# Attention steps of a transformer layer on one core: projections placed earlier, one sum of four key tiles in place of two sums of pairs, the shift behind a pair block

## The chip, the core and the metric

One core of a Trainium2 chip runs the kernel as one program. The metric is the device time in microseconds. TensorE (PE) multiplies matrices, VectorE (DVE), ScalarE (ACT) and GpSimd (POOL) do elementwise work, SyncE (SP) issues most transfers. Each engine has a queue of its own and works it off in order; they wait for each other by semaphores.

## The reference

```python
# x: 2 x 1024 x 512; 16 heads of 32; FF = 2048
qkv = einsum('bsd,ed->bse', x, w_qkv) + b_qkv
scores = einsum('bhqd,bhkd->bhqk', q, k) / sqrt(32) + causal
out = einsum('bhqk,bhkd->bhqd', softmax(scores), v) @ w_out.T + b_out
x = layernorm(x + out)
hidden = relu((x @ sign(up_w).T) * up_scale)
x = layernorm(x + (hidden @ sign(down_w).T) * down_scale * output_scale)
```

## The kernel before

The attention goes in 8 steps (`STEPS`): a step is one group of four heads of one batch, so that step s is batch s % 2, group s // 2. In a step there are 48 score tiles (`PIECES`): for each half f of the queries (512), each key tile j of 128, each of the four heads h. Piece n = 4g + h belongs to key-tile group g; groups 0 to 3 are the first half, 4 to 11 the second. Groups 4 to 7 are full tiles of 512 columns; those of 0 to 3 and 8 to 11 touch the diagonal, narrow from 512 to 128 columns and are masked.

For every piece PE writes scores into PSUM (L983), ACT takes the exponential into a ring of 14 tiles, `probs` (L681), GpSimd masks diagonal tiles (L594). Per group, PE multiplies the four tiles with V (`pv`, L1013) and with ones for the row sums (`sum`, L1007); these use 32 columns of the array each, four heads side by side, and a pair of groups makes a "pair block". For groups 4 to 7 GpSimd first adds tiles in pairs (`add`, L601: groups 4+5 into `pairs`, then 6+7) and PE sums the pairs (`sum_added`, L991): two blocks of four heads per step. VectorE then divides (`norm`, L805 a reciprocal, L807 a product), and the second half's first `pv` (group 4) waits for the first half's division.

Softmax needs a maximum per row beforehand. For step s+1, 48 unit scores (`max`, L946) are computed during step s, into three banks `ps_unit`, and reduced by VectorE: units 16 to 31 by L783 (512 columns each), the others by L779 with the causal mask. Unit n waits until unit n-3 is reduced. The maxima are turned by PE (`shift`, L957), ACT and VectorE split them into a high and low part (L666, L793), SyncE lays them as two rows beside K for the scores of step s+1.

Q and K of a coming step come from 4 projections of 12 matmuls (`proj`, L906), in fp32r with values split into a high and a low part: `PARTS` lists weight and input part of the three passes. In steps from 2 on every projection goes into one bank, `ps_proj`. ACT copies it out twice (`full` L654, `high` L660), GpSimd forms the low part (L588), SyncE stores and reloads. The first matmul of a projection waits until `high` of the one before is done. In even steps VectorE and GpSimd also prepare the weights of the next group (L767, L567).

What sets the order on all engines is one list written out by hand, `plan()`. Every job has a slot; 48 slots make a step, and slot t+n is score n. All engines walk the same sorted list, each taking its own kinds of jobs. `PAIRED` and `ALONE` (last two steps) place the groups, `MAXIMA` the unit scores, `BLOCK` and `LAST_BLOCK` the projections: (steps ahead, projection, first slot, slots between matmuls, slots of evict, keep and fill). The score of piece n waits until the exponential of piece n-2 is done, since there are two score banks.

In the last step PE also begins the output projection (`attn`, L1029); the feed-forward part (L1056, L1073) begins behind the last scores.

The waits of the parts that the prediction walks through:

```python
# PE, proj
if m == 0:
    wait(pe, s_qk, NB * s + k - (s == 0 or s == 1 and k == 1))
# PE, max
wait(pe, s_max, NU * s + n - 2)
# ACT, shift
act.wait_ge(s_mt, 2 * s + n + 1)
# ACT, high
nc.scalar.activation(parts[:, k % 2, 0, :], proj_bank(s, n)[:, :], ...).then_inc(s_qk, 1)
# PE, pv
if what == "pv" and j == 0:
    wait(pe, s_norm, QT * s + 4 * f)
```

## Time and profile before

| | |
|---|---|
| three runs | 795.46, 795.60, 797.47 us, median 795.6 |
| profiled execution, its own time | 801.23 us |
| its span, first to last instruction | 799.5 us |
| mean granted clock of TensorE | 0.974 |
| PE, DVE, ACT, POOL busy | 746.0, 456.0, 323.2, 345.9 us |
| shares of the chain that ended last | PE 75%, DVE 15%, issue 4% |

In a timeline row the first number is the start from the beginning of the span, the second how long the merged instructions lasted, then engine, line, operation, what is written and read, the shape and the count; in brackets the idle time of the engine just before and who ended it. Ends of matmuls are modelled, so starts are what to go by.

### The profile page before, as it was taken

To read this page: it belongs to the slowest core of one execution; us is meant where nothing else is said; L and a number is where in the kernel's file an instruction comes from. 1 tells how busy PE (TensorE), PEld (TensorE's weight loads), DVE (VectorE), ACT (ScalarE), POOL (GpSimd) and SP (SyncE) were. 2 spreads that over 40 slices of the span, in tenths; PEclk is the share of its full clock that TensorE was granted. 3 is DMA by queue.
4 is the path that set the end of the run, shared out by engine and by line. 5 is a ranking of instruction groups with operands and counts; after the bars stand their busy time and mean duration, and the time that the engine had idled before them with its cause. 6 is when DMAs were issued, how large, how long until landed. Compare 5 with 4: busy or idle time off the path is not lost.

```text
span 799.5 us, 11694 instructions
## 1 busy us (share of the span) xinstructions
PE 746.0 (93%) x4048; PEld 509.6 (64%) x4048; DVE 456.0 (57%) x1086; ACT 323.2 (40%) x631; POOL 345.9 (43%) x479
## 2 busy tenths in 40 slices
PE   6899899999999999999989897999999999999994
PEld 4687655655556455555554453588778877878882
DVE  3276386676766767758576662433277329433614
ACT  5111355555555655545555556532231223221220
POOL 4441456364553555544527534362244234323333
PEclk9999899999999999999997997999999999999998
DMA  6966263525545344344467440413002101000101
GB/s 233 311 166 184 68 178 114 146 81 144 156 112 157 95 134 145 92 145 124 130 188 219 145 162 5 155 43 119 14 14 105 27 14 39 14 1 2 52 1 52
DMA packets 44619, 85.71 MB, mean 107 GB/s; under 512 B 4880, under 2 KB 13584, under 8 KB 44432
## 3 DMA queue, kind: packets, MB, share of 16 engines
q1 hardware_dynamic: 35536, 79.72, 33.1%
q10 hardware_dynamic: 9024, 5.24, 2.3%
q8 instruction: 32, 0.52, 0.3%
q14 instruction: 27, 0.22, 0.1%
HBM read 55.33 MB, written 29.36 MB: 106 GB/s over the span
## 4 chain that ended last, share of the span: by engine, by line
PE 75%; DVE 15%; issue 4%; ACT 2%; DMA 2%; POOL 2%; ACTq 0%; SPq 0%; POOLq 0%; DVEq 0%
PE ps_heads L1013 9%; PE ps_unit L946 9%; PE ps_proj L906 8%; DVE heads_sb L805 7%; PE ps_proj L1056 7%; PE ps_score L983 6%; PE ps_score L1073 6%; PE ps_unit L1029 6%; PE ps_unit L1056 5%; PE ps_sum L1007 5%; PE ps_heads L1073 3%; PE ps_sum L1073 3%; DVE maxes L783 2%; PE ps_sum L991 2%; DVE heads_sb L807 2%
## 5 line engine op out<-in xcount | busy, mean ns | idle before, releaser
L681 ACT ACTIVATE probs<-ps_score 128x512 f32<-128x512 f32 (+3 forms) x360 | 170.8, 490 | 180.1 <-PE ps_score L983 171.3
L779 DVE CUSTOM_DVE_ANT_0 ps_unit<-ps_unit,causal 128x128 f32<-128x128 f32 (+3 forms) x256 | 121.9, 512 | 77.0 <-PE ps_unit L946 74.3
L625 POOL TENSOR_TENSOR hid_low<-hid_raw,hid_high 128x512 fp32r<-128x512 f32 x64 | 85.0, 1328 | 174.6 <-DVE hid_high L856 171.5
L946 PE MATMUL ps_unit<-stack 96*128 96x512 f32 (+3 forms) x384 | 134.4, 364 | 10.9 <-DVE maxes L783 4.3
L983 PE MATMUL ps_score<-stack 98*128 98x512 f32 (+2 forms) x360 | 134.9, 383 | 7.5 <-ACT probs L681 6.0
L594 POOL TENSOR_SCALAR_AFFINE_SELECT probs<-probs 128x128 f32<-128x128 f32 x256 | 73.9, 294 | 153.6 <-ACT probs L681 150.9
L946 PEld LDWEIGHTS ps_unit<-stack 96*128 96x128 f32 x384 | 72.6, 193 | 57.3 <-issue 17.4
L856 DVE CAST hid_high<-hid_raw 128x512 fp32r<-128x512 f32 x64 | 27.1, 424 | 131.1 <-ACT hid_raw L736 130.9
L783 DVE TENSOR_REDUCE maxes<-ps_unit 128x1 f32<-128x512 f32 x128 | 80.7, 684 | 26.0 <-PE ps_unit L946 25.6
L983 PEld LDWEIGHTS ps_score<-stack 98*128 98x128 f32 x360 | 69.3, 195 | 40.6 <-ACT probs L681 23.9
L1013 PE MATMUL ps_heads<-probs,v_rows 128*32 128x512 f32 (+3 forms) x768 | 84.5, 511 | 5.1 <-DVE heads_sb L807 3.3
L601 POOL TENSOR_TENSOR pairs<-probs 128x512 f32<-128x512 f32 x64 | 79.9, 1278 | 10.2 <-ACT probs L681 9.4
L805 DVE RECIPROCAL heads_sb<-ps_sum 128x128 f32<-128x128 f32 x64 | 60.8, 950 | 12.1 <-PE ps_sum L1007 12.1
L588 POOL TENSOR_TENSOR parts<-qk_full,parts 128x512 fp32r<-128x512 f32 x32 | 41.1, 1283 | 57.2 <-ACT parts L660 57.2
L736 ACT ACTIVATE hid_raw<-ps_proj,up_scale 128x512 f32<-128x512 f32 x32 | 22.0, 688 | 93.0 <-PE ps_proj L1056 93.0
L906 PE MATMUL ps_proj<-x_high,w_high 128*128 128x512 f32 x116 | 46.0, 425 | 6.5 <-ACT x_high L638 6.5
L1073 PE MATMUL ps_score<-down_sb,hid_high 128*128 128x512 f32 x124 | 50.1, 404 | 0.0
L1007 PE MATMUL ps_sum<-probs,ones 128*32 128x128 f32 (+3 forms) x512 | 49.4, 441 | 0.0
L1073 PE MATMUL ps_score<-down_sb,hid_low 128*128 128x512 f32 x124 | 48.9, 395 | 0.0
L906 PE MATMUL ps_proj<-x_low,w_high 128*128 128x512 f32 x116 | 45.3, 417 | 0.0
L1013 PEld LDWEIGHTS ps_heads<-probs,v_rows 128*32 128x32 f32 x768 | 19.6, 110 | 39.6 <-issue 24.8
L906 PE MATMUL ps_proj<-x_high,w_low 128*128 128x512 f32 x116 | 44.7, 416 | 0.0
(184 smaller groups left out, 1208.1 us busy)
## 6 DMA issues: line engine op xcount, KB each, us to landing
stack<-qk_parts SPq DMA_DIRECT2D x96, 256.0 KB, 4.7
qk_parts<-parts SPq DMA_DIRECT2D x32, 512.0 KB, 2.7
v_all<-h_even ACTq DMA_DIRECT2D x16, 256.0 KB, 3.4
v_rows<-v_all SPq DMA_DIRECT2D x8, 512.0 KB, 4.5
heads_t<-heads_sb SPq DMA_DIRECT2D x16, 256.0 KB, 2.6
raw<-up_w SPq DMA_DIRECT2D x8, 512.0 KB, 3.6
x_tile<-x_rows SPq DMA_DIRECT2D x16, 256.0 KB, 5.0
raw<-down_w SPq DMA_DIRECT2D x8, 512.0 KB, 3.8
```

What stands on the lines that cost most here:

```text
L625: nc.gpsimd.tensor_tensor(hid[1][:, (HM * s + n) % 3, :], hid_raw[:, n % 2, :], hid[0][:, (HM * s + n) % 3, :].bitcast(FP32), ALU.subtract ...
L681: nc.scalar.activation(probs[:, (NP * s + n) % RING, 0:width], score_bank(s, n)[:, off:off + width], ACT.Exp, scale=SCALE).then_inc(s_exp, 1)
L779: nc.vector.tensor_tensor_reduce(ps_unit[n % 3][:, 0:width], ps_unit[n % 3][:, 0:width], causal[:, HALF - width:], 1.0, NEG, ALU.add, ALU.max,
L783: nc.vector.tensor_reduce(maxes[:, 1, col:col + 1], ps_unit[n % 3][:, :], AXIS_X, ALU.max).then_inc(s_max, 1)
L805: nc.vector.reciprocal(heads_sb[:, cols], ps_sum[:, cols]).then_inc(s_rc, 1)
L906: mm = nc.tensor.matmul(proj_bank(s, k)[:, :], ws[wp][:, c, t, :], xs[xp][:, c, t0:t0 + HALF], start=(m == 0), stop=(m == 11))
L946: nc.tensor.matmul(ps_unit[n % 3][:, 0:width], stack[s % 2][0:96, 1, f, h, i % 4 * P:(i % 4 + 1) * P], stack[s % 2][0:96, 0, c, h, 0:width ...
L983: nc.tensor.matmul(score_bank(s, n)[:, 0:width + off], stack[s % 2][0:98, 0, j // 4, h, j % 4 * P:(j % 4 + 1) * P], stack[s % 2][0:98, 1, ...
L1007: nc.tensor.matmul(ps_sum[rows, at:at + width], ones[:, :], tile, **args).then_inc(s_pv, 1)
L1013: mm = nc.tensor.matmul(ps_heads[rows, at:at + width], v_rows[:, s % 2, j, rows], tile, **args)
L1056: mm = nc.tensor.matmul(ps_up[n % 2][:, :], up_sb[n // 8][:, n % 8, m % DC, :], turned[s % 2][m // DC][:, m % DC, :], start=(m == 0), stop ...
L1073: mm = nc.tensor.matmul(ps_down[i][:, :], hid[part][:, (HM * s + n) % 3, i * P:(i + 1) * P], down_sb[:, down_at(n), :], start=(n == 0 and ...
```

## The change

Projections (1, 2) and (2, 0) begin at slots 0.5 and 20.5 instead of 4.2 and 22, with more room between their matmuls. From step 1 on, the pass with the weights' low part is the last of three. The unit scores 16 to 18 start at slot 26.3 instead of 25.2, and those behind them are spread anew. The shift moves from 35.9 to 36.02, behind the pair block at 36, and stays ahead of `full` at 36.05. In steps 0 to 5 GpSimd adds groups 4 to 7 into one set of four tiles, `added`, in 12 instructions from slot 21.7 on, and PE sums them in one block at slot 43.9, which now starts the sum of the second half. Steps 6 and 7 have no adds: groups 4 to 7 are summed directly there, each beside its `pv`.

```diff
--- before.py
+++ after.py
@@ -39,17 +39,19 @@
 ALONE_NORM = [[18.4, 18.41, 18.42, 18.43, 50.4, 50.41, 50.42, 50.43],
               [17.6, 17.61, 17.62, 17.63, 48.7, 48.71, 48.72, 48.73]]
 
-MAXIMA = ([10.2 + 0.55 * u for u in range(5)] + [13.4 + 0.55 * u for u in range(11)]
-          + [25.2 + 0.6 * u for u in range(5)] + [28.4 + 0.7 * u for u in range(27)])
-BLOCK = [(1, 2, 4.2, 0.72, 13.05, 15.8, 18.5), (1, 3, 13.3, 0.5, 19.65, 22.4, 24.8),
-         (2, 0, 22, 1.1, 36.05, 38.8, 41.3), (2, 1, 36.3, 0.6, 44.05, 46.8, 49.2)]
-LAST_BLOCK = [(1, 2, 4.2, 0.48, 9.9, 12.5, 14.9), (1, 3, 11.9, 0.45, 17.1, 19.9, 22.2)]
+MAXIMA = ([10.4 + 0.5 * u for u in range(5)] + [13.4 + 0.55 * u for u in range(11)]
+          + [26.3 + 0.6 * u for u in range(3)] + [28.4 + 0.53 * u for u in range(14)] + [37.5 + 0.66 * u for u in range(15)])
+BLOCK = [(1, 2, 0.5, 0.98, 13.05, 15.8, 18.5), (1, 3, 13.3, 0.5, 19.65, 22.4, 24.8),
+         (2, 0, 20.5, 1.25, 36.05, 38.8, 41.3), (2, 1, 36.3, 0.6, 44.05, 46.8, 49.2)]
+LAST_BLOCK = [(1, 2, 0.5, 0.78, 9.9, 12.5, 14.9), (1, 3, 11.9, 0.45, 17.1, 19.9, 22.2)]
 
 
 FIRST_ADD, LAST_ADD = 4, 8
-NA = 2 * GH
+NA = 3 * GH
+ADDING = STEPS - 2
 
 
 UNITS = [(h, i, c) for f in range(2) for c in range(f + 1) for h in range(GH) for i in range(4 * f, 4 * f + 4)]
@@ -141,12 +143,12 @@
         paired = s < STEPS - 2
         for g, at in enumerate(PAIRED if paired else ALONE[s % 2]):
             put(t + at, "pv", s, g)
-            if g < FIRST_ADD or g >= LAST_ADD:
+            if g < FIRST_ADD or g >= LAST_ADD or s >= ADDING:
                 put(t + at, "sum", s, g)
-        for a in range(2):
-            for h in range(GH):
-                put(t + 25.6 + 8 * a + 0.01 * h, "add", s, GH * a + h)
-            put(t + (33, 41)[a], "sum_added", s, a)
+        if s < ADDING:
+            for a in range(NA):
+                put(t + 21.7 + 1.3 * a, "add", s, a)
+            put(t + 43.9, "sum_added", s)
         for q, at in enumerate(PAIRED_NORM if paired else ALONE_NORM[s % 2]):
             put(t + at, "norm", s, q)
             if q % 4 == 3:
@@ -154,7 +156,7 @@
         if s + 1 < STEPS:
             for u, at in enumerate(MAXIMA):
                 put(t + at, "max", s + 1, u)
-            put(t + 35.9, "shift", s + 1, 0)
+            put(t + 36.02, "shift", s + 1, 0)
             put(t + 47.2, "row_max", s + 1, 1)
             put(t + (51.9 if s + 2 < STEPS else 48.2), "shift", s + 1, 1)
             put(t + 17, "v_rows", s + 1)
@@ -274,8 +276,8 @@
         s_mask = sem("probs_masked")
         s_pv = sem("probs_used")
         s_rc = sem("row_sum_inverted")
-        s_add = sem("prob_pairs_added")
-        s_used = sem("prob_pairs_used")
+        s_add = sem("probs_added")
+        s_used = sem("added_probs_used")
         s_norm = sem("heads_normalized")
         s_st = [sem(f"heads_stored{f}") for f in range(2)]
         s_raw = [sem(f"raw_weights_loaded{i}") for i in range(2)]
@@ -337,7 +339,7 @@
         stack1 = sb(left, "stack1", [P, 2, 2, GH, HALF], FP32R)
         stack = [stack0, stack1]
         probs = sb(left, "probs", [P, RING, HALF], FP32)
-        pairs = sb(left, "pairs", [P, GH, HALF], FP32)
+        added = sb(left, "added", [P, GH, HALF], FP32)
         v_rows = sb(left, "v_rows", [P, 2, QT, P], FP32)
         heads_sb = sb(left, "heads_sb", [P, HALF], FP32)
         causal = sb(left, "causal", [P, HALF], BF16)
@@ -594,12 +596,17 @@
                     nc.gpsimd.affine_select(out=tile, in_=tile, compare_op=ALU.is_ge, fill=0.0, base=0,
                                             pattern=[[1, P]], channel_multiplier=-1).then_inc(s_mask, 1)
                 if what == "add":
-                    k = NP * s + GH * (FIRST_ADD + n // GH * 2) + n % GH
-                    pool.wait_ge(s_exp, k + GH + 1)
-                    wait(pool, s_used, NA * s + n - GH + 1)
-                    nc.gpsimd.tensor_tensor(pairs[:, n % GH, :], probs[:, k % RING, :], probs[:, (k + GH) % RING, :],
-                                            ALU.add).then_inc(s_add, 1)
+                    h = n % GH
+                    k = NP * s + GH * (FIRST_ADD + 1) + n
+                    pool.wait_ge(s_exp, k + 1)
+                    if n < GH:
+                        wait(pool, s_used, GH * s - GH + h + 1)
+                        other = probs[:, (k - GH) % RING, :]
+                    else:
+                        pool.wait_ge(s_add, NA * s + n - GH + 1)
+                        other = added[:, h, :]
+                    nc.gpsimd.tensor_tensor(added[:, h, :], other, probs[:, k % RING, :], ALU.add).then_inc(s_add, 1)
                 if what == "sign" and n < 2:
 
                     pool.wait_ge(s_sign, n + 1)
@@ -676,8 +683,8 @@
 
                     wait(act, s_pv, NP * s + n - RING + 1)
                     k = n - RING - GH * FIRST_ADD
-                    if 0 <= k < 2 * NA:
-                        act.wait_ge(s_add, NA * s + k // (2 * GH) * GH + k % GH + 1)
+                    if s < ADDING and 0 <= k < GH * (LAST_ADD - FIRST_ADD):
+                        act.wait_ge(s_add, NA * s + (k if k < GH else k - GH) + 1)
                     nc.scalar.activation(probs[:, (NP * s + n) % RING, 0:width], score_bank(s, n)[:, off:off + width],
                                          ACT.Exp, scale=SCALE).then_inc(s_exp, 1)
                 if what == "sign":
@@ -889,7 +896,7 @@
                 if what == "proj":
                     k, m = n // 12, n % 12
                     t, f = PROJ[k]
-                    (wp, xp), c = PARTS[m // DC], m % DC
+                    (wp, xp), c = PARTS[m // DC if m < DC or s == 0 else 3 - m // DC], m % DC
                     b, g = s % 2, s // 2
                     t0 = b * SEQ + f * HALF
                     if b == 0 and k == 0 and m == 0:
@@ -987,8 +994,8 @@
                 if what == "sum_added":
                     for h in range(GH):
                         rows = slice(h * HD, (h + 1) * HD)
-                        pe.wait_ge(s_add, NA * s + GH * n + h + 1)
-                        nc.tensor.matmul(ps_sum[rows, :], ones[:, :], pairs[:, h, :], start=(n == 0), stop=False,
+                        pe.wait_ge(s_add, NA * s + NA - GH + h + 1)
+                        nc.tensor.matmul(ps_sum[rows, :], ones[:, :], added[:, h, :], start=True, stop=False,
                                          tile_position=(0, h * HD)).then_inc(s_used, 1)
                 if what in ("pv", "sum"):
                     f, j, _ = PIECES[GH * n]
@@ -1011,7 +1018,7 @@
                         else:
                             pe.wait_ge(s_exp, NP * s + k + 1)
                         mm = nc.tensor.matmul(ps_heads[rows, at:at + width], v_rows[:, s % 2, j, rows], tile, **args)
-                        if FIRST_ADD <= n < LAST_ADD:
+                        if s < ADDING and FIRST_ADD <= n < LAST_ADD:
                             mm.then_inc(s_pv, 1)
                 if what == "attn":
                     i, m = n // 12, n % 12
```

## Rows read from the trace of the kernel before

**Rows 1.** The page, busy time of each engine (share of span, instructions).

```profile
PE 746.0 (93%) x4048; PEld 509.6 (64%) x4048; DVE 456.0 (57%) x1086; ACT 323.2 (40%) x631; POOL 345.9 (43%) x479
```

**Rows 2.** Windows: us, then busy of each engine, clock, DMA share, GB/s.

```profile
98.00:149.10 51.10, 48.39 (x326) 28.66 (x322) 36.28 (x101) 27.72 (x59) 26.93 (x48) 1.00 0.47 135
404.70:455.00 50.30, 43.81 (x250) 22.91 (x247) 34.26 (x91) 26.46 (x52) 25.14 (x36) 0.88 0.64 205
455.00:505.00 50.00, 43.88 (x262) 22.35 (x261) 20.38 (x37) 28.71 (x54) 19.72 (x36) 0.88 0.23 76
416.00:419.50 3.50, 2.14 (x5) 0.74 (x4) 3.40 (x7) 3.29 (x7) 0.49 (x1) 1.00 0.72 291
419.50:429.80 10.30, 9.62 (x29) 4.68 (x30) 5.20 (x11) 4.14 (x8) 7.66 (x5) 0.50 0.71 204
498.00:501.40 3.40, 3.37 (x12) 1.08 (x12) 0.00 (x0) 0.00 (x0) 0.95 (x4) 0.50 0.00 0
```

**Rows 3.** Timeline of TensorE, step 3 and start of step 4: start us, us, line.

```profile
261.50 0.73 PE L983 MATMUL ps_score<-stack 98*128 98x512 f32 x2
...
267.22 0.50 PE L946 MATMUL ps_unit<-stack 96*128 96x512 f32 x1 [0.71 <-DVE maxes L783]
...
268.48 1.92 PE L1013 MATMUL ps_heads<-probs,v_rows 128*32 128x512 f32 x16
...
274.32 1.07 PE L991 MATMUL ps_sum<-pairs,ones 128*32 128x512 f32 x8
...
278.03 0.28 PE L957 MATMUL ps_unit<-ident,maxes 128*16 128x128 f32 x1 [0.56 <-DVE maxes L783]
...
278.42 1.92 PE L1013 MATMUL ps_heads<-probs,v_rows 128*32 128x512 f32 x16
...
280.43 0.45 PE L906 MATMUL ps_proj<-x_high,w_high 128*128 128x512 f32 x1
...
287.51 1.07 PE L1013 MATMUL ps_heads<-probs,v_rows 128*32 128x512 f32 x8
...
293.17 0.99 PE L983 MATMUL ps_score<-stack 98*128 98x512 f32 x2 [0.26 <-ACT probs L681]
...
295.64 0.44 PE L983 MATMUL ps_score<-stack 98*128 98x384 f32 x1
...
301.03 0.50 PE L946 MATMUL ps_unit<-stack 96*128 96x512 f32 x1 [0.30 <-DVE maxes L779]
```

**Rows 4.** Timeline of ScalarE, the same stretch.

```profile
262.03 3.46 ACT L681 ACTIVATE probs<-ps_score 128x512 f32<-128x512 f32 x6
...
278.40 0.27 ACT L666 ACTIVATE shift_h<-ps_unit 16x128 fp32r<-16x128 f32 x1 [0.54 <-PE ps_unit L957]
...
279.52 0.66 ACT L660 ACTIVATE parts<-ps_proj,bias_sb 128x512 fp32r<-128x512 f32 x1
```

**Rows 5.** Timeline of VectorE, the same stretch.

```profile
266.48 3.07 DVE L783 TENSOR_REDUCE maxes<-ps_unit 128x1 f32<-128x512 f32 x5
270.87 4.42 DVE L783 TENSOR_REDUCE maxes<-ps_unit 128x1 f32<-128x512 f32 x7 [1.32 <-PE ps_unit L946]
...
293.00 0.17 DVE L789 TENSOR_TENSOR row_max<-maxes 128x16 f32<-128x16 f32 x1
...
300.63 0.29 DVE L779 CUSTOM_DVE_ANT_0 ps_unit<-ps_unit,causal 128x128 f32<-128x128 f32 x1
```

**Rows 6.** Timeline of GpSimd in step 7.

```profile
492.75 4.99 POOL L601 TENSOR_TENSOR pairs<-probs 128x512 f32<-128x512 f32 x4
```

**Rows 7.** Timeline of TensorE in step 6.

```profile
420.18 1.94 PE L1013 MATMUL ps_heads<-probs,v_rows 128*32 128x512 f32 x8 [1.62 <-DVE heads_sb L807]
```

**Rows 8.** Timeline of TensorE in step 7.

```profile
498.03 1.30 PE L1013 MATMUL ps_heads<-probs,v_rows 128*32 128x512 f32 x2 [1.74 <-POOL probs L594]
```

**Rows 9.** Timeline of all engines, end of step 6.

```profile
450.80 1.26 POOL L619 TENSOR_TENSOR x_tile<-x_tile,b_out_sb 128x512 f32<-128x512 f32 x1
450.87 1.23 DVE L789 TENSOR_TENSOR row_max<-maxes 128x16 f32<-128x16 f32 x1
```

## The prediction

> **What bounds it now.** I read the page first: TensorE is busy 93% of the span [rows 1]. So a change pays only where it shortens TensorE's queue, or a wait in front of it. By stretches, the eight attention steps fall in two kinds [rows 2]: steps 0 to 5 take 51.1 us each, PE busy 48.4 of it at full clock; step 6 (404.7 to 455) and step 7 (455 to 505) have PE busy 44 of 50 at a mean clock of 0.88. The feed-forward half behind 507 us isn't touched. Everything below is therefore one period of step 3, walked along TensorE's timeline, times the number of steps, and then steps 6 and 7 by themselves. Slots are those of plan(); slot 20 of step 3 is at 261.50, slot 28's pair block at 268.48, slot 36's at 278.42, slot 44's at 287.51, slot 52's ends at 295.64 [rows 3].
>
> What the reader is to see in that walk is who ends each wait. From 261.50 to 268.48 (6.98 us) scores go at ScalarE's pace, six exponentials in 3.46 us [rows 4], and then a maximum waits 0.71 for VectorE, which has only just finished the division (its first reduce starts at 266.48) [rows 3, 5]. At 278.03 the shift waits 0.56 for VectorE. Between 287.51 and 302 it is ScalarE at 293.17 and VectorE at 301.03 [rows 3].
>
> **The change, part by part, one period.**
>
> Sums. A block of column sums of the added tiles takes 1.07 us at 274.32 [rows 3]; with a slower matmul on both sides I take 1.2 for it (bounds 1.0 and 1.3). Two blocks become one in steps 0 to 5: 1.2 less. GpSimd gets twelve adds for eight; four take 4.99 us [rows 6], so 15.0 us, begun at slot 21.7 and over by slot 36 to 38. The block at slot 43.9 (some 286 us) and the exponentials 30 to 45, which reuse the tiles, come later, so this costs nothing; if GpSimd were late, each add behind its need would cost 1.25. The projection parts behind them on its queue and on SyncE's go out at about the time they do now.
>
> Slots 20 to 28. Two maxima leave this stretch and the first comes 1.1 slots later, so the 0.71 is gone. ScalarE's chain stays: seven exponentials at 0.577 from 262.03 end at 266.1. The first projection now sits behind score 20 and must wait for the bank until ScalarE's copy, just ahead of 262.03, is done, which holds score 21 back 0.3 or so. The pair block then starts at about 267.0 instead of 268.48: 1.5 less (bounds 1.0 and 2.0). In even steps the weight copy and the low weights come ahead of this as before; passing them last only makes them due later, and I cost it at nothing; without that cover it would be one short wait per group.
>
> Slots 28 to 36. TensorE comes to the maxima with only three done. Thirteen reduces of 0.63 (seven take 4.42, [rows 5]) are left, 8.2 us, against about 6.7 us of matmuls. VectorE has an idle stretch under the pair block, its next reduce starts near 269.7, and the last but one of the maxima is let in at about 276.1. Slot 36's block starts near 277.05, so this stretch is 10.0 us against 9.94: the sum block's 1.2 and the 0.56 are eaten by waits for VectorE.
>
> Slots 36 to 44. Here lies what decides. The shift now comes behind the pair block (1.85 us), at about 278.9. ScalarE has one queue in the same order: shift_h, then the copy of the finished projection (36.05), then its high part (36.1). Now these run under the pair block: 278.40, and the high part from 279.52 for 0.66, and the next projection's first matmul is at 280.43, just after [rows 3, 4]. After the change that first matmul stands right behind the shift, and waits for the same bank. From shift to the end of the high part is 0.37+0.18+0.57+0.7, so 1.9 us with the signal, of which 0.2 is the shift's own: 1.7 us of TensorE doing nothing (bounds: nothing, if something else had held it anyway, and 2.0). Behind it are scores 37 on, all in order. The rest, 7.08 from 280.43 to 287.51, loses one maximum (0.23). So 1.85+1.9+6.95 against 9.09: 1.6 more.
>
> Slots 44 to 61. One maximum of 512 columns has moved in here (0.23), and the third after it waits for its reduce of 0.63, about 0.3 more. Four projections fill the gaps between scores 0 to 3; those are latency gaps of about 0.9 in all, so they cost some 0.3: 0.8 more up to slot 52. From the end of slot 52's block the division and the next unit on VectorE set the time: the fourth maximum comes 5.39 after it (295.64 to 301.03, VectorE's unit from 300.63) [rows 3, 5] however little stands in between. Taking four projections out of that stretch only makes a larger hole; one fewer behind it gives 0.24. Net 0.55 more (bounds −0.5 and 1.2).
>
> Sum: −1.5+0.1+1.6 = +0.2 for slots 20 to 44, six times, +1.2; +0.55 five times, +2.8. At the start of step 0 there is no division, so there the fill is a true gain of about 0.9.
>
> Step 6. Its entry has five projections ahead of the slot-52 block, +1.1 by the same walk. It regains direct sums, four blocks; the first two fall where the clock is at 1.2 GHz (one block of eight took 1.94 there, [rows 7]) and cost 1.9 each, the others half of that, 0.9, less 2.4 for the two added sums: +3.2 if TensorE has no room, 0 if all of it goes into waits for VectorE. I take 1.8. Step 7: the first direct sum lies in a wait, the other three cost 3.6 (1.9, 0.9 and 0.9, rounded down); 2.4 goes; and the masks no longer stand behind four adds [rows 6]: the 1.74 at 498.03 goes [rows 8], and with it, if the clock stays up, half of the 3.4 us at clock 0.50 behind it [rows 2], 1.7. With 0.2 of smaller slack that is −2.4 (3.6−2.4−1.7−1.7−0.2; bounds 0 and −5).
>
> All: +1.2+2.8−0.9+2.9−2.4 = **+3.6 us**. The profiled execution took 801.2 (span 799.5); that is 5.6 above the median of the runs, 795.6. I carry the difference over: 799.2.
>
> **Rivals.** (a) *The bank wait doesn't show.* If the first matmul behind the shift isn't held, six times 1.7 = 10.2 goes, and 789.0 is left: faster. For it: the other terms of the period, a block and two VectorE waits, are visible gains. Against: ScalarE's order and the bank are the plan's own. It decides at the gap between shift and next projection; below 1.1 us the whole is faster than before. (b) *The clock falls.* It fell behind 416 to 419.5, where PE had little to do, and stood at 0.50 for 10.3 us [rows 2]. The holes ahead of the fourth maximum and behind the shift are each 1.5 to 1.7 long; now no steady step loses its clock. The shortest stretch at 0.50, 498.0 to 501.4, costs half its length, 1.7; one such in each of six steps gives 809. It decides if PE's work around a hole gets as thin as there. (c) *Gains and losses cancel*: the small terms (0.3s and 0.2s) come out 0.6 less per step, and the time is 795.6. (d) *VectorE blocked by the adds.* A row_max took 1.23 us beside a GpSimd add, and 0.17 alone [rows 5, 9]; were it caught in each of six steps, 1.06 each, 805.6. Against: the adds end ten slots before it, and reduces took 0.61 to 0.63 beside adds and without.
>
> The Trainium skill, "SBUF — State Buffer", section "Who interferes with whom", has a rule that speaks against more GpSimd adds: a VectorE instruction with two SBUF inputs and a GpSimd instruction that reads SBUF shut each other out for the whole instruction, while a tensor_reduce never does. By that rule the sum stays as it is unless row_max drifts into the adds, and then it is (d)'s; the trace agrees, both in the long row_max and in the even reduces.
>
> **Numbers.** Forecast as summed: 0.43, its own range 795 to 803, a fifth of it within 0.3% of before. (a) 0.30; (b) 0.14; (c) 0.11; (d) 0.02. A change under 0.3% (2.4 us) can't be told from none. Faster 0.30; within 0.3%: 0.20; slower 0.50. The range, from (a) with some more of step 7 to (b): 786 to 809.
>
> **What would show it.** Right: after slot 36's block a shift, then an idle time of TensorE of 1.5 to 1.9 us ended by ScalarE's high part; one L991 block a step; no wait at slot 26; waits for L783 spread over slots 29 to 35; a hole before the fourth maximum of over 1 us; a period of 51.7 to 52.1 us; step 7 without the mask wait. Wrong: a period at or below 50.5, or the projection starting within 0.5 us of the shift; also clock falls before 400 us.

## The result and the profile after

The changed kernel takes **803.3 us** (median of 4 runs, 802.42 to 803.91), the kernel before 795.77 in the same comparison (795.46 to 797.47): ratio 1.0089, 95% interval [1.0067, 1.0112]. It is 0.9% slower. The forecast was 799.2 in a range of 786 to 809, slower with 0.50: right in its sign and inside its range, 4.1 us too low.

The profiled executions stand closer together: 803.83 (span 802.1) against 801.23 (span 799.5). The page after, busy time of each engine:

```profile
PE 744.5 (93%) x4032; PEld 503.6 (63%) x4032; DVE 451.1 (56%) x1086; ACT 322.9 (40%) x631; POOL 356.5 (44%) x487
```

PE is *less* busy than in [rows 1], by 1.5 us and 16 instructions, and the kernel is slower: the loss is waiting. Windows after (us, busy of each engine, clock, DMA share, GB/s), of step 0, step 3, steps 6 and 7, then of the three low stretches in them:

```profile
86.70:136.20 49.50, 46.78 (x282) 27.38 (x283) 29.91 (x89) 27.44 (x57) 33.53 (x52) 1.00 0.42 124
239.90:291.70 51.80, 48.45 (x316) 28.22 (x315) 35.21 (x100) 27.77 (x58) 29.22 (x48) 1.00 0.42 123
395.40:457.50 62.10, 54.18 (x332) 26.33 (x331) 38.43 (x105) 31.82 (x64) 18.35 (x37) 0.90 0.59 184
457.50:509.60 52.10, 46.78 (x306) 25.07 (x304) 21.60 (x41) 31.81 (x62) 12.35 (x33) 0.92 0.25 82
404.40:407.90 3.50, 3.26 (x16) 0.60 (x16) 0.83 (x5) 0.12 (x1) 1.41 (x3) 0.52 0.58 221
421.50:428.30 6.80, 5.25 (x20) 1.69 (x21) 2.54 (x6) 2.14 (x4) 2.35 (x1) 0.51 0.79 211
455.60:465.90 10.30, 9.03 (x47) 5.44 (x40) 3.15 (x9) 3.74 (x7) 5.09 (x8) 0.51 0.06 14
```

The same windows of before for steps 0, 6 and 7:

```profile
87.00:138.60 51.60, 48.93 (x290) 30.01 (x290) 30.65 (x88) 27.51 (x57) 28.23 (x48) 0.93 0.39 115
394.20:450.00 55.80, 51.27 (x316) 27.12 (x315) 38.76 (x105) 32.12 (x64) 27.75 (x46) 0.91 0.67 208
450.00:507.20 57.20, 48.46 (x290) 25.00 (x288) 22.64 (x41) 31.98 (x62) 22.59 (x43) 0.88 0.22 74
```

Cut at the first score of each step (read off TensorE's timeline; step 7 ends at its last score), the difference of the two profiled executions is:

| | step 0 | steps 1 to 5, all | step 6 | step 7 |
|---|---|---|---|---|
| before | 51.68 | 255.57 | 55.79 | 57.21 |
| after | 49.46 | 259.22 | 62.12 | 52.09 |
| difference | −2.2 | +3.65 | +6.3 | −5.1 |
| forecast | −0.7 | +3.75 | +2.9 | −2.4 |

(Steps 1 to 5 of the forecast are +0.75 each, 0.2+0.55; step 0 is 0.2−0.9; step 6 is 1.1+1.8.) The steady steps came out as forecast, the three odd ones with the right sign and at half the size or less. What the forecast's walk through step 3 named stands in TensorE's timeline after:

```profile
275.68 0.39 PE L990 MATMUL ps_score<-stack 98*128 98x384 f32 x1
276.00 1.92 PE L1020 MATMUL ps_heads<-probs,v_rows 128*32 128x512 f32 x16
277.86 0.28 PE L964 MATMUL ps_unit<-ident,maxes 128*16 128x128 f32 x1
279.69 0.73 PE L913 MATMUL ps_proj<-x_high,w_high 128*128 128x512 f32 x2 [1.56 <-ACT parts L667]
...
285.30 1.06 PE L998 MATMUL ps_sum<-added,ones 128*32 128x512 f32 x8
```

Against [rows 3]: the shift (now L964) stands behind the pair block, and behind it TensorE does nothing for 1.56 us until ScalarE has made the high part. There is one block of added sums (L998) for two. ScalarE's timeline shows the queue that does it:

```profile
278.23 0.27 ACT L673 ACTIVATE shift_h<-ps_unit 16x128 fp32r<-16x128 f32 x1 [1.62 <-PE ps_unit L964]
278.41 0.66 ACT L661 ACTIVATE qk_full<-ps_proj,bias_sb 128x512 f32<-128x512 f32 x1
278.98 0.66 ACT L667 ACTIVATE parts<-ps_proj,bias_sb 128x512 fp32r<-128x512 f32 x1
```

ScalarE itself waits 1.62 for the shift's transpose, with two finished projection tiles to copy queued behind. VectorE's timeline of the same stretch:

```profile
265.67 1.88 DVE L790 TENSOR_REDUCE maxes<-ps_unit 128x1 f32<-128x512 f32 x3
268.73 7.87 DVE L790 TENSOR_REDUCE maxes<-ps_unit 128x1 f32<-128x512 f32 x13 [1.19 <-PE ps_unit L953]
```

Three reduces before the pair block, thirteen behind it, as the walk had it ([rows 5]: five and seven). And in the page's list of costliest groups the wait is one row:

```profile
L913 PE MATMUL ps_proj<-x_high,w_high 128*128 128x512 f32 x116 | 46.2, 424 | 16.2 <-ACT parts L667 9.3
```

9.3 us of it ended by L667, six times 1.55.

### The profile page after: what moved, and what is told of

Same layout as the page of the kernel before. It is cut to its first block, busy times and chain, and to the rows that moved or that the text cites. A ratio compares the mean times of both kernels' runs of the same rounds, so it can differ in the third digit from the quotient of the medians.

```text
span 802.1 us, 11678 instructions
## 1 busy us (share of the span) xinstructions
PE 744.5 (93%) x4032; PEld 503.6 (63%) x4032; DVE 451.1 (56%) x1086; ACT 322.9 (40%) x631; POOL 356.5 (44%) x487
## 4 chain that ended last, share of the span: by engine, by line
PE 76%; DVE 12%; issue 4%; ACT 3%; DMA 2%; POOL 1%; SPq 0%; ACTq 0%; DVEq 0%; POOLq 0%
PE ps_heads L1020 9%; PE ps_unit L953 9%; PE ps_proj L913 8%; PE ps_score L990 7%; PE ps_proj L1063 7%; PE ps_score L1080 6%; PE ps_unit L1036 6%; PE ps_sum L1014 5%; PE ps_unit L1063 5%; DVE heads_sb L812 4%; PE ps_heads L1080 3%; PE ps_sum L1080 3%; DVE maxes L790 2%; PE ps_sum L933 1%; PE ps_score L933 1%
## 5 line engine op out<-in xcount | busy, mean ns | idle before, releaser
L688 ACT ACTIVATE probs<-ps_score 128x512 f32<-128x512 f32 (+3 forms) x360 | 170.3, 491 | 183.1 <-PE ps_score L990 176.3
L953 PE MATMUL ps_unit<-stack 96*128 96x512 f32 (+3 forms) x384 | 133.7, 366 | 14.5 <-DVE maxes L786 10.2
L1020 PE MATMUL ps_heads<-probs,v_rows 128*32 128x512 f32 (+3 forms) x768 | 82.0, 505 | 4.3 <-DVE heads_sb L814 4.3
L609 POOL TENSOR_TENSOR added<-added,probs 128x512 f32<-128x512 f32 x48 | 60.5, 1274 | 0.0
L1014 PE MATMUL ps_sum<-probs,ones 128*32 128x512 f32 (+3 forms) x576 | 58.0, 468 | 0.0
L743 ACT ACTIVATE hid_raw<-ps_unit,up_scale 128x512 f32<-128x512 f32 x32 | 21.9, 685 | 52.8 <-PE ps_unit L1063 52.8
```

What stands on the lines that cost most here:

```text
L688: nc.scalar.activation(probs[:, (NP * s + n) % RING, 0:width], score_bank(s, n)[:, off:off + width], ACT.Exp, scale=SCALE).then_inc(s_exp, 1)
L953: nc.tensor.matmul(ps_unit[n % 3][:, 0:width], stack[s % 2][0:96, 1, f, h, i % 4 * P:(i % 4 + 1) * P], stack[s % 2][0:96, 0, c, h, 0:width ...
L1014: nc.tensor.matmul(ps_sum[rows, at:at + width], ones[:, :], tile, **args).then_inc(s_pv, 1)
L1020: mm = nc.tensor.matmul(ps_heads[rows, at:at + width], v_rows[:, s % 2, j, rows], tile, **args)
```

## The experiments

Each was timed beside the kernel before (medians 795.3 to 796.0 over 16 to 29 runs). Step lengths are those of its profiled execution. Rows of different comparisons are best set against each other by their ratios.

| kernel | us | ratio to before | step 0 | steps 1 to 5, mean | step 6 | step 7 |
|---|---|---|---|---|---|---|
| before | 795.77 | 1 | 51.68 | 51.11 | 55.79 | 57.21 |
| after | 803.3 | 1.0089 [1.0067, 1.0112] | 49.46 | 51.84 | 62.12 | 52.09 |
| e1_shift_late | 793.49 | 0.9953 [0.9926, 0.9980] | 48.04 | 50.42 | 59.63 | 53.46 |
| e2_proj_back | 805.77 | 1.0103 [1.0066, 1.0139] | 52.09 | 52.07 | 62.00 | 52.22 |
| e3_only_shift | 802.35 | 1.0076 [1.0049, 1.0104] | 52.31 | 51.99 | 54.41 | 57.00 |
| e4_only_sums | 790.3 | 0.9918 [0.9883, 0.9954] | 49.61 | 50.31 | 56.29 | 53.47 |
| e5_sums_maxima | 799.04 | 1.0030 [1.0001, 1.0060] | 50.90 | 51.23 | 61.06 | 52.38 |
| e6_sums_fill | 791.54 | 0.9931 [0.9904, 0.9959] | 47.78 | 50.28 | 56.39 | 53.46 |
| e7_parts_back | 803.15 | 1.0098 [1.0070, 1.0126] | 49.48 | 51.84 | 61.58 | 52.64 |
| e9_maxima_back_6 | 791.82 | 0.9937 [0.9911, 0.9963] | 48.03 | 50.42 | 57.80 | 51.83 |
| e11_shift_back | 792.61 | 0.9955 [0.9932, 0.9979] | 49.04 | 50.41 | 61.95 | 51.78 |
| e10_even_maxima | 797.13 | 1.0000 [0.9973, 1.0026] | 50.24 | 51.08 | 59.57 | 52.93 |
| e12_fill_wait | 794.16 | 0.9968 [0.9944, 0.9992] | 47.78 | 50.25 | 59.56 | 53.47 |

### The shift: the wait behind it

The changed kernel, with the shift a few places later, behind the copies' slots 36.05 and 36.1:

```diff
-            put(t + 36.02, "shift", s + 1, 0)
+            put(t + 36.2, "shift", s + 1, 0)
```

> The changed kernel with one slot altered: the shift at 36.2, behind ScalarE's two copies of the projection (36.05 and 36.1) and still ahead of the next projection (36.3). Theory (bank wait): TensorE's wait of 1.56 us for ScalarE's high part goes in each of steps 0 to 5, the period falls from 51.8 to about 50.3 us, and the time from 803.3 to 794 (792 to 796), at or below the kernel before. Rival (the wait is only passed on, to the shift's own chain or to VectorE, which stands at the maxima anyway): under 3 us are won, time above 800, and a new wait of over 1 us stands behind the pair block or ahead of score 48.

793.49 us. ScalarE now copies while the pair block runs, and in TensorE's timeline the projection follows the shift at once; all that is left is 0.15 for VectorE:

```profile
273.85 1.92 PE L1020 MATMUL ps_heads<-probs,v_rows 128*32 128x512 f32 x16
275.71 0.28 PE L964 MATMUL ps_unit<-ident,maxes 128*16 128x128 f32 x1
275.74 0.71 PE L913 MATMUL ps_proj<-x_high,w_high 128*128 128x512 f32 x2
...
276.78 0.39 PE L953 MATMUL ps_unit<-stack 96*128 96x256 f32 x1 [0.15 <-DVE shift_l L800]
```

A position in a list, 0.18 of a slot, is worth 9.8 us by the medians (1.4% by the two ratios, whose intervals lie far apart), and more than the whole loss; in the profiled executions 8.5 us of it lie in steps 0 to 5, 1.42 in each. The same slot put alone into the kernel before:

```diff
-            put(t + 35.9, "shift", s + 1, 0)
+            put(t + 36.02, "shift", s + 1, 0)
```

> The kernel before with the shift at 36.02 in place of 35.9 and nothing else. Theory (bank wait): the wait of 0.56 for VectorE ahead of the shift goes, and a wait of 1.5 to 1.7 for ScalarE's high part comes behind it: 0.9 to 1.1 more in each of steps 0 to 5, period 52.1, time 795.8 + 6 = 802 (800 to 803). Rival (the pair block hides the shift and nothing waits): 0.5 less per step, 792 to 793.

802.35 us, in the middle of what was expected, 6.3 more than the kernel before beside it; and the wait stands in its timeline too:

```profile
277.48 1.92 PE L1013 MATMUL ps_heads<-probs,v_rows 128*32 128x512 f32 x16
279.33 0.28 PE L957 MATMUL ps_unit<-ident,maxes 128*16 128x128 f32 x1
281.17 0.50 PE L906 MATMUL ps_proj<-x_high,w_high 128*128 128x512 f32 x1 [1.50 <-ACT parts L660]
```

Here the period grows by 0.88 only, since the wait for VectorE ahead of the shift (0.56 in [rows 3]) goes in return. In the changed kernel there is hardly such a wait to win (with the shift ahead of the block, below, it sums to 1.3 us over six steps), and so taking the bank wait out gives 1.42 a step.

### The sums alone

The changed kernel with MAXIMA, BLOCK, LAST_BLOCK, the order of the passes and the shift as before: only the twelve adds, the one block at slot 43.9 and the direct sums in steps 6 and 7 are new.

```diff
-            put(t + 36.02, "shift", s + 1, 0)
+            put(t + 35.9, "shift", s + 1, 0)
...
-                    (wp, xp), c = PARTS[m // DC if m < DC or s == 0 else 3 - m // DC], m % DC
+                    (wp, xp), c = PARTS[m // DC], m % DC
```

(and the three lists of slots back to those of before.)

> The kernel before with the sums alone changed: twelve adds and one block per step in steps 0 to 5, direct sums in steps 6 and 7; projections, maxima and shift stand as before. Theory (VectorE's reduces take a part of the saved block back): of the 1.2 us of a block 0.7 to 0.9 is won per step, period 50.3, step 6 some 2 longer, step 7 some 2 to 4 shorter, time 790 (788 to 793). Rival 1 (GpSimd's twelve adds are late, and score exponentials or the block at slot 43.9 wait for them): 796 or more, with waits for L609. Rival 2 (TensorE alone counts): 1.2 per step, 787 or less.

790.3 us, as expected: **the sums alone make the kernel 0.8% faster than before.** The period falls by 0.9 in steps 2 to 5 (50.2 for 51.1), by 0.5 in step 1. All of it lies between slots 28 and 36, 9.03 us for 9.93: the block that goes (1.07 in [rows 3]), less 0.14 that the wait for VectorE ahead of the shift grows (0.7 for 0.56). Its windows of steps 3, 6 and 7:

```profile
235.00:285.20 50.20, 47.38 (x315) 28.43 (x316) 35.67 (x100) 27.73 (x58) 29.19 (x49) 1.00 0.44 127
385.70:442.00 56.30, 50.48 (x331) 25.68 (x331) 38.42 (x106) 32.01 (x65) 17.99 (x39) 0.97 0.65 209
442.00:495.40 53.40, 46.73 (x309) 24.74 (x306) 22.81 (x43) 31.39 (x60) 13.31 (x34) 0.94 0.23 78
```

Step 6 is only 0.5 longer than before, but at a clock of 0.97 for 0.91. At 1.2 GHz it spent 3.4 us here and 10.2 before; half of the 6.8 less is 3.4, so at the same clock the direct sums cost step 6 up to 3.9 us. Step 7 is 3.7 shorter, 3.4 of which such a count gives to the clock too (6.8 us low for 13.6).

### The projection at the start of a step

```diff
-BLOCK = [(1, 2, 0.5, 0.98, 13.05, 15.8, 18.5), (1, 3, 13.3, 0.5, 19.65, 22.4, 24.8),
+BLOCK = [(1, 2, 4.2, 0.72, 13.05, 15.8, 18.5), (1, 3, 13.3, 0.5, 19.65, 22.4, 24.8),
...
-LAST_BLOCK = [(1, 2, 0.5, 0.78, 9.9, 12.5, 14.9), (1, 3, 11.9, 0.45, 17.1, 19.9, 22.2)]
+LAST_BLOCK = [(1, 2, 4.2, 0.48, 9.9, 12.5, 14.9), (1, 3, 11.9, 0.45, 17.1, 19.9, 22.2)]
```

> The changed kernel with projection (1, 2) begun at slot 4.2 again, in all steps. Theory (the division on VectorE sets slots 52 to 61): the hole of 1.26 us ahead of the fourth maximum shrinks to 0.3, the stretch from slot 44 to 61 loses 0.5 in steps 1 to 5 and 1.1 at step 6's entry, step 0 loses its gain of 0.9: 803.3 less 3, so 800 (798 to 802). Rival (the fill is a true gain, since it uses time in which scores wait for exponentials): the time rises by 3 to 6, to 806 to 809.

805.77 us: neither as expected; it lies nearer the rival's 806, but the two ratios overlap (1.0103 and 1.0089), and the rival's reason would show in every step. The projections' new place does not cost the steady steps (51.76 to 51.86 in four of the five, as after), so my theory of 0.5 a step falls. Step 0 loses what the fill gave it (52.09 for 49.46), and step 3 took 53.07 by a fall of the clock at its start. The window:

```profile
244.90:248.30 3.40, 3.40 (x35) 1.75 (x35) 0.42 (x2) 1.04 (x3) 0.69 (x3) 0.55 0.82 219
```

The next two kernels are the one with the sums, each with one more edit. With the fill (slot 4.2 to 0.5, both lists):

> The kernel with the new sums alone (790.3 us), with the projection of slot 4.2 begun at slot 0.5 in every step and the maxima, the other blocks and the shift as before. Theory (the fill pays only where nothing else ends the wait, in step 0): step 0 goes from 49.6 to about 48.0 us and loses its stretch of low clock, steps 1 to 5 stay at 50.25, steps 6 and 7 stay at 109.8: 788.7 (787.5 to 790). Rival (the fill is what costs in steps 6 and 7): these take 3 us more, 792 (791 to 793.5).

Steps as the theory had them (step 0 at 47.78, no low stretch in it; steps 1 to 7 unchanged), but the median, 791.54, lies above the expected 787.5 to 790 and can't be told from that of the sums alone: the intervals overlap almost wholly. The profiled execution, 788.08, was the best of its ten. With the maxima's new slots instead:

> The kernel with the new sums alone (790.3 us), with the maxima's new slots added to it and nothing else. Theory (the maxima's new slots are what costs steps 6 and 7): the steady period goes from 50.25 to about 50.5 us, five times 0.25 is 1.2, and steps 6 and 7 together go from 109.8 to about 113, so 790.3 + 1.2 + 3.2 = 794.7 (793 to 797). Rival (steps 6 and 7 lose by the projections filled in between the first scores, or by a clock fall that has nothing to do with the maxima): steps 6 and 7 stay within 1 us of 109.8, and the time is 790 to 792.

799.04 us, more than either expected. Steps 6 and 7 together rose to 113.4, as the theory said. But steps 1, 2 and 4 took 51.8 to 51.9, and steps 3 and 5 took 50.3: three of five began with a fall of the clock. The window of the first, then the 3.4 us ahead of it, and the same stretch of step 3, where no fall followed:

```profile
137.40:140.80 3.40, 3.26 (x35) 1.60 (x34) 0.28 (x1) 1.45 (x4) 0.88 (x3) 0.57 0.58 144
134.40:137.80 3.40, 2.70 (x10) 1.43 (x10) 2.71 (x11) 2.19 (x6) 1.33 (x5) 1.00 0.52 175
238.00:241.40 3.40, 2.70 (x10) 1.43 (x10) 2.69 (x11) 2.21 (x6) 1.35 (x5) 1.00 0.70 208
```

What TensorE did ahead of the first, in its timeline:

```profile
135.18 0.75 PE L952 MATMUL ps_unit<-stack 96*128 96x384 f32 x2 [0.38 <-DVE maxes L785]
135.77 2.43 PE L989 MATMUL ps_score<-stack 98*128 98x256 f32 x5
138.00 0.41 PE L963 MATMUL ps_unit<-ident,row_max 128*16 128x128 f32 x1
```

The merged row carries the shape of its first score alone: it is the last score of step 0 (256 columns) and the first four of step 1 (512 each). From the second on they start 0.53 to 0.64 us apart, while a matmul of 512 columns right behind another of 512 starts 0.24 behind it (281.60 and 281.84 in the changed kernel), so TensorE in part waits in them, though the row counts as busy. Then the full set of parts, with the shift alone where it was:

```diff
-            put(t + 36.02, "shift", s + 1, 0)
+            put(t + 35.9, "shift", s + 1, 0)
```

> The changed kernel with the shift alone back at slot 35.9, ahead of the pair block. Against the kernel with the new sums and the new maxima (799.0 us) it differs by the projections filled in at slot 0.5, by the first projection at slot 20.5 and by the order of the passes. Theory (the fill keeps PE fed at the start of a step, and so the clock up): no stretch of low clock at 136, 188 or 291 us, all of steps 1 to 5 at 50.4, step 0 at 48: 799.0 less 1.5 for each of four falls and less 1.3 of step 0 is 792 (790 to 794). Rival (the falls come with the maxima's new slots whatever stands at slot 0.5): periods of 51.8 in some of steps 1 to 5 again, and 796 to 800.

792.61 us, and steps 1 to 5 all at 50.35 to 50.48, with no low stretch in any. Step 0 did have one, 3.4 us at 87.9, and took 49.04 for the 48 expected: in step 0 the fill doesn't rule a fall out. The same place in its timeline has the projections between the scores:

```profile
134.72 0.52 PE L990 MATMUL ps_score<-stack 98*128 98x256 f32 x2
135.07 0.40 PE L913 MATMUL ps_proj<-x_high,w_high 128*128 128x512 f32 x1
135.36 0.50 PE L990 MATMUL ps_score<-stack 98*128 98x512 f32 x1
135.70 0.39 PE L913 MATMUL ps_proj<-x_high,w_high 128*128 128x512 f32 x1
```

So the fill is worth nothing in time where the clock holds, and 1.5 us a step where it would fall. The two kernels differ also in the first projection at 20.5 and the order of the passes; the run that differs from the changed kernel by the fill alone (e2_proj_back) had one fall in its five steady steps. Counted over all profiled executions: with the maxima's new slots and no fill, four of ten steady steps began with a fall; with these slots and the fill, none of 25; with the old slots and no fill, none of 20. In these executions a fall took both, the new slots and the missing fill; what in the slots brings it isn't shown.

### The maxima in step 6

```diff
-            for u, at in enumerate(MAXIMA):
+            for u, at in enumerate(MAXIMA if s + 2 < STEPS else LAST_MAXIMA):
```

with the shift at 36.2 and LAST_MAXIMA the list of before.

> The changed kernel with the shift at slot 36.2 (793.5 us), and in step 6 alone the maxima at their old slots. Theory (the maxima's new slots cost step 6 some 3.1 us between its slots 32 and 48, where VectorE also splits the attention's output in parts, and nothing in steps 1 to 5): step 6 takes 56.5 instead of 59.6, steps 1 to 5 stay at 50.4, step 7 at 53.5: 790.3 (789 to 792). Rival (step 6 is longer by its projections, or by where its clock falls): step 6 stays over 58.5 and the time at 792 to 795.

791.82 us, inside the expected range; step 6 takes 57.80 for 59.63. Both kernels have a low stretch of 6.8 us in that step, so this 1.8 is not the clock: from slot 28 to the end it is 24.9 us for 26.8. The size is 1.8 and not the 3.1 I had expected, and the medians' 1.7 lies within the noise of both intervals; the direction is the theory's. TensorE's waits from slot 28 of step 6 on, with the new slots (shift at 36.2):

```profile
PE ps_unit L953 <- DVE maxes L786: 2.5, 3, 1.2
PE ps_unit L953 <- DVE shift_l L800: 0.6, 1, 0.6
```

and with the old ones in that step:

```profile
PE ps_unit L955 <- DVE maxes L788: 1.5, 2, 1.3
PE ps_unit L955 <- DVE shift_l L802: 0.8, 1, 0.8
```

One wait of 1.0 for VectorE is visible; the rest of the 1.8 is not in the named waits.

### The order of the passes

```diff
-                    (wp, xp), c = PARTS[m // DC if m < DC or s == 0 else 3 - m // DC], m % DC
+                    (wp, xp), c = PARTS[m // DC], m % DC
```

> The changed kernel with the low weights' pass back in its old place, in the middle, in every step. Theory (the order of the three passes is worth nothing, since the low weights are ready long before either order needs them): the time of the changed kernel, 803.3 (801.5 to 805), and the same step lengths. Rival (the low weights came late in the old order): a wait of TensorE for GpSimd or VectorE ahead of the second pass in even steps, 0.5 us or more each, 805 to 808.

803.15 us, the changed kernel's time, with the same steady steps: the order is worth nothing, as costed.

### The kernel before once more

> The kernel before, unchanged, for a second profile of it. Theory (the first profiled execution, 801.2 us, was an unlucky one by its clock: stretches at half clock at 88, 420, 454, 481 and 498 us): this execution lies at 795 to 797, with less time at half clock in steps 0, 6 and 7, and steps 1 to 5 at 51.1 as before. Rival (profiling itself costs this kernel some 5 us): 801 again, with the same stretches.

803.36 us at a clock of 0.972. My theory fell: this execution has the same low stretches from step 0 to step 7 as the first, to their lengths (among them 6.8 us at 90, 10.2 at 421, 6.8 at 483), and the same step lengths to 0.04. How common that is, another comparison shows: of its 29 runs of before the median is 795.38 at a clock of 0.981, and seven lie between 800.39 and 802.32 at 0.974 to 0.976; over the four comparisons of the experiments 11 of 88 lie above 800. Two such in two may be chance or may be the profile; that is open. For other kernels the profiled execution lies on either side of their median (796.22 for 793.49, 788.08 for 791.54). What counts is the consequence, below.

### Two versions that were to beat both kernels

The sums with the fill, and in steps 0 to 5 an even pitch for the maxima, none ahead of slot 26.3:

```diff
-          + [25.2 + 0.6 * u for u in range(5)] + [28.4 + 0.7 * u for u in range(27)])
+          + [26.3 + 0.6 * u for u in range(3)] + [28.4 + 0.65 * u for u in range(29)])
```

> A version that might beat both kernels: the new sums, the projection begun at slot 0.5, the shift ahead of the pair block, in steps 0 to 5 the two maxima out of slots 25 and 26 and the rest at an even pitch of 0.65, in step 6 the old maxima. Theory (a maximum before slot 26.3 waits for VectorE's division, and the old pitch has slack to take the two): 0.2 to 0.5 us less per step than the kernel with sums and fill (791.5), so 788 to 791. Rival (VectorE's reduces end the stretch 20 to 36 in either order): the same as that kernel, 791.5 within 1.

797.13 us: a miss beyond the rival. The period rises from 50.28 to 51.08. In step 3 it is 1.3 us ahead at slot 28 of the kernel with sums and fill, has lost 1.2 of it at slot 36, and loses 1.0 more between slots 44 and 48. At slot 36 it is the shift that waits for VectorE:

```profile
PE ps_unit L966 <- DVE maxes L792: 1.3, 1, 1.3
```

(0.7 with the old slots.) With the change's own list, 0.53 up to slot 35.3, that wait is 0.2 a step (the 1.3 over six steps told above), and yet slot 36 comes no earlier there: 36.10 us behind the step's first score, for 36.12 here. Up to that slot the rival has it, VectorE's reduces end the stretch in either order. The even pitch loses to the change's list behind it, 0.35 up to slot 44 and 0.2 after. Most of the miss, the loss of 1.0 behind slot 44, isn't the pitch's own: from slot 44 to the next step's slot 20 every kernel with maxima held back takes 25.9 us or more, and those with the old list 25.1. It wasn't traced further than to the waits for maxima, two of 1.6 us in all for one of 1.1.

The other, with step 6's second projection spread into the wait for the division:

```diff
-LAST_BLOCK = [(1, 2, 0.5, 0.78, 9.9, 12.5, 14.9), (1, 3, 11.9, 0.45, 17.1, 19.9, 22.2)]
+LAST_BLOCK = [(1, 2, 0.5, 0.78, 9.9, 12.5, 14.9), (1, 3, 12, 0.98, 23, 25.5, 28)]
```

> The kernel with the new sums and the fill at slot 0.5 (791.5 us), with step 6's second projection spread over slots 12 to 23 instead of 12 to 17 and its copy, parts and rows later to match, so that it stands where TensorE waits for scores and, ahead of slot 24's block, 1.6 us for VectorE's division. Theory (TensorE's work moved into a wait is gained, and a wait filled keeps the clock up): step 6 loses 1.5 us or more of its 56.4 and the fall at 409 us goes or shrinks: 789.5 (787 to 790.5). Rival (VectorE and ScalarE end this stretch whatever TensorE does, and the projections only move its wait): step 6 stays at 56 to 57 and the time at 791 to 792.5.

794.16 us. Step 6 got 0.8 shorter up to slot 28, then lost 4.0, up to 1.7 of it by a low stretch of 3.4 us at 437. ScalarE's waits from slot 28 to the end of step 6:

```profile
ACT probs L688 <- PE ps_score L990: 6.4, 5, 2.0
ACT up_a L701 <- DMA raw<-up_w: 6.0, 3, 3.0
```

0.2 of the second before. In SyncE's queue the stack's stores wait behind GpSimd's low part, 5.1 us for 2.5:

```profile
SPq L519 <- PE ps_proj L913: 6.6, 1, 6.6
SPq L76 <- POOL parts L590: 5.1, 1, 5.1
```

The first load of weights (L519) waits by the plan for the last projection, which was moved: 6.6 us for 3.2. The loads of the feed-forward weights are issued from the same queue behind the stack's stores, ScalarE stands at its head waiting for these, and with it the exponentials: TensorE then waits 2.2 us for L688, where it waited nothing there. A move of twelve matmuls came back through that wait and two in-order queues; how much each of them costs wasn't tested apart.

Of the versions that are faster than both kernels the three fastest are the sums alone (0.9918), the sums with the fill (0.9931) and the changed kernel with the shift at 36.2 and the old maxima in step 6 (0.9937). Their intervals overlap; none is shown to be the best.

## Why the prediction was right, and where its sizes were off

What decided, the bank wait behind the shift, was forecast by its cause and its size, and two runs show it. That the forecast's total came near the profiled pair's, +3.6 for +2.6, is partly luck: step 6 was forecast 3.4 us too low, and the gains of steps 0 and 7 were 1.5 and 2.7 too small.

**Slots 20 to 28**, −1.5: right. From slot 20's score to slot 28's block it is 5.41 us for 6.98.

**Slots 28 to 36**, +0.1: right, 9.90 for 9.94. The sum block and the 0.56 were eaten by VectorE's thirteen reduces, as walked.

**Slots 36 to 44**, +1.6: right, 10.61 for 9.09, with a bank wait of 1.56 in it. (By its own terms it should read +1.5, since 7.08 less 0.23 is 6.85 and not 6.95.) This is the step that decided, and rival (a) (789.0 without the wait) falls: the wait is there. The run that removes it shows what (a) would have been, 793.5 and not 789.0; its price of 10.2 us was right (9.8), and the difference is the 4.1 us by which the whole forecast was low.

**Slots 44 to 61**, +0.55: size right (+0.77 by the timelines), a part of the reason wrong. I charged the four projections with 0.3 of it; moved back, they leave it as it is (25.87 us from slot 44 to the next step's slot 20, where the clock holds, for 25.90), and put into the kernel with the sums they add nothing (25.14 for 25.12). The charge belongs to the maxima: their new slots alone, added to the sums, make it 25.87. The hole ahead of the fourth maximum came as said, 1.10 us.

**The sums**, −1.2 a step: −0.9 by the run that has them alone. The block was 1.07 and not 1.2, and 0.14 went to the wait for VectorE ahead of the shift. By the runs with parts of the change, a steady step is made up of −0.9 for the sums, +0.1 for the maxima and the early first projection, nothing for the fill and the order of the passes, and +1.4 for the shift's place.

**Step 0**, −0.7: −2.2. I had the gain of the fill as filled time, and the clock there as given. The clock was at 1.2 GHz from 88.4 to 95.2 in before and not once in that step after; the run without the fill has the low stretch back and 52.09. All six executions without the fill have a low stretch of 3.4 or 6.8 us in step 0, of the eight with it two have one, of 3.4. This was the term "a true gain of about 0.9".

**Step 6**, +2.9: +6.3, the largest error. Two sizes failed. "I take 1.8" for the direct sums, between 0 and 3.2, was the middle where even the upper end was passed: up to 3.9 at equal clock, in a stretch where scores already wait. And nothing was charged for the maxima's new slots, though the list holds in step 6 too and VectorE also splits the output there: 1.8. The entry, +1.1, isn't visible: with the fill alone step 6 takes 56.39 for 56.29. Clock: 12.1 us low for 10.2, at most 1 us. The prediction also took steps 6 and 7 as the windows from 404.7 and from 455, some 50 us each; by their first scores they begin at 394.2 and 450.0 and take 55.79 and 57.21. No term of its sum rests on that.

**Step 7**, −2.4: −5.1. The mask's wait went, as said. The clock gave up to 2.6 and not 1.7 (13.6 us at 1.2 GHz before, 8.4 after). What was missed stands in TensorE's waits of that step, before:

```profile
PE ps_unit L1040 <- DVE h_even L845: 2.3, 1, 2.3
PE ps_unit L957 <- DVE row_max L789: 1.8, 1, 1.8
PE ps_heads L1013 <- POOL probs L594: 1.7, 1, 1.7
```

and after:

```profile
PE ps_unit L1047 <- DVE h_even L852: 1.4, 1, 1.4
PE ps_unit L964 <- DVE row_max L796: 0.4, 1, 0.4
```

The wait for h_even is 0.9 shorter with the sums alone too. The row_max that took 1.23 beside a GpSimd add [rows 9] now takes 0.18, and its wait shrinks by 1.4. I had that row and used it only for rival (d), as a thing that could get worse. The maxima's slots don't explain it, since the run with the shift at 36.2 has them too, and there row_max takes 1.23 and TensorE waits as before:

```profile
PE ps_unit L964 <- DVE row_max L796: 1.8, 1, 1.8
```

What goes with it in all 14 profiled executions is the clock. In the six where TensorE stood at 1.2 GHz at the first score of step 7 (the changed kernel among them), row_max starts 0.03 us ahead of the GpSimd add and takes 0.18. In the eight where it stood at 2.4 GHz, row_max starts 0.06 to 0.07 us behind the add and takes 1.23. So a low stretch that lies across that start would give back a part of what it costs; this was not tested by itself. By the Trainium skill ("SBUF — State Buffer", section "Who interferes with whom") a VectorE instruction with two SBUF inputs and a GpSimd one that reads SBUF keep each other out, a reduce not. The trace agrees on both: row_max 1.23 behind the add for 0.18 ahead of it, and thirteen reduces in 7.87, 0.61 each, beside adds.

**The base.** The sum was made against the profiled execution (801.2) and 5.6 carried over to the median. The profile pair shows +2.6, near the +3.6 of the sum; the medians +7.5. The clocks explain the gap: the profiled run of before had 0.974, its median run 0.981 to 0.983, while the changed kernel has 0.980 in its profile and 0.980 to 0.982 in every run. What step 0 and step 7 gain in the pair by a steadier clock, the median run of before had for the most part already. A forecast should have asked which of its gains are gains of clock, and left those out of the median.

**Rival (b)**, the clock falls in steady steps, didn't come in the changed kernel, but it is real: two of its parts together (sums and maxima) bring it, three steps in five, at 1.5 each, and in no steady step with the fill did it come. **Rival (d)** didn't come either: row_max took 0.16 to 0.18 us in all eight steps.

## What to carry to other kernels

Where one engine serves two kinds of small work from one in-order queue, the *place* of an instruction among its neighbours decides: an item put just ahead of a copy that frees a bank makes the copy wait for everything the item waits for. Before moving an item, list what stands within half a slot of it on every engine, DMA queues too. And when a profiled run stands apart from the median, read its clock before carrying its difference over.

## What had not been expected of the hardware

In the kernel with sums and maxima TensorE was counted busy for 2.70 of the 3.40 us ahead of a fall to 1.2 GHz in step 1, and for the same 2.70 us in step 3, with the same row of scores, where the clock stayed at 2.4. With four matmuls of 512 columns between those scores it stayed at 2.4 in all 25 steady steps that have them together with the maxima's new slots. The busy share of a window doesn't tell whether the clock will hold.

The clock also differs from run to run of one binary: for the kernel before 0.972 to 0.987, with times from 803.4 to 793.2 us, a spread of 1.3% and larger than the effect that was studied. Only a ratio over many runs beside each other could tell the parts of this change apart.
